# Causal attention in a macaron block: diagonal maxima as packed banks, and q and k loaded in two steps

## The reference

```
scores = jnp.einsum('bhsd,bhtd->bhst', q, k) * scale
causal = jnp.triu(jnp.ones((S, S), dtype=bool), k=1)
scores = jnp.where(causal, -jnp.inf, scores)
probs = jax.nn.softmax(scores, axis=-1)
out = jnp.einsum('bhst,bhtd->bhsd', probs, v)
```

## Time and profile before

| what | us |
|---|---|
| median of 3 runs (1600.67 to 1618.32) | 1615.71 |
| the profiled execution | 1608.4 |
| its span, first to last instruction | 1606.7 |
| PE busy, 8384 matmuls | 1381.6 |
| DVE busy | 1139.5 |
| ACT busy | 860.6 |
| plain maxima on DVE (L1026), 768 | 490.8 |
| masked maxima on DVE (L1031), 512 | 238.3 |
| finds on PE (L1112), 1280 | 478.9 |
| scores on PE (L1133), 1280 | 327.3 |
| products on PE (L1150), 2560 | 322.4 |
| exponentials on ACT (L1001), 640 | 542.7 |

### The profile page before, as it was taken

How to read it: one execution, slowest core, us unless ns; L and a number is a source line. 1 busy time by engine, 2 the same in 40 slices (tenths; PEclk the granted TensorE clock), 3 DMA queues, 4 the chain that set the end, 5 groups by cost and what they waited for, 6 DMA issues and landing times. The chain is left out here.

```text
span 1606.7 us, 27137 instructions
## 1 busy us (share of the span) xinstructions
PE 1381.6 (86%) x8384; PEld 821.8 (51%) x8384; DVE 1139.5 (71%) x2689; ACT 860.6 (54%) x1155; POOL 229.9 (14%) x206
## 2 busy tenths in 40 slices
PE   5988888750799999999999989999999976899997
PEld 5877777640443343343343333433433422799986
DVE  5666676821788888877887887888888930567675
ACT  5644444310036666655665665666666655466564
POOL 0012222346001011010010110110110101110100
PEclk9999999875568899997997999999999978899999
DMA  5113333437152062070080260440620002222312
GB/s 204 40 40 105 105 118 100 150 123 95 13 69 34 6 83 24 5 101 8 9 98 5 30 82 5 55 52 6 72 34 5 8 8 68 92 80 92 95 51 66
DMA packets 101898, 97.86 MB, mean 61 GB/s; under 512 B 46288, under 2 KB 85200, under 8 KB 100048
## 3 DMA queue, kind: packets, MB, share of 16 engines
q1 hardware_dynamic: 101744, 95.98, 29.0%
HBM read 57.15 MB, written 37.75 MB: 59 GB/s over the span
## 5 line engine op out<-in xcount | busy, mean ns | idle before, releaser
L1001 ACT ACTIVATE probs<-s_ps 128x1024 f32<-128x1024 f32 (+3 forms) x640 | 542.7, 895 | 327.7 <-PE s_ps L1133 326.4
L1112 PE MATMUL m_ps<-kT,qT 64*128 64x512 f32 (+3 forms) x1280 | 478.9, 478 | 112.9 <-DMA qT<-qkT_parts 55.9
L1026 DVE TENSOR_REDUCE maxes<-m_ps 128x1 f32<-128x512 f32 x768 | 490.8, 684 | 48.5 <-PE m_ps L1112 44.2
L1112 PEld LDWEIGHTS m_ps<-kT,qT 64*128 64x128 f32 x1280 | 217.2, 201 | 502.2 <-DVE maxes L1026 274.0
L1133 PE MATMUL s_ps<-qT,kT 64*128 64x512 f32 (+3 forms) x1280 | 327.3, 416 | 13.8 <-DMA qT<-shiftT 10.5
L1031 DVE CUSTOM_DVE_ANT_0 masked<-m_ps,mask_b 128x384 f32<-128x384 f32 (+3 forms) x512 | 238.3, 488 | 130.6 <-PE m_ps L1112 125.0
L1150 PE MATMUL o_ps<-probs,v_w 128*32 128x512 f32 (+3 forms) x2560 | 322.4, 578 | 0.2 <-POOL probs L974 0.2
L974 POOL TENSOR_SCALAR_AFFINE_SELECT probs<-probs 128x512 f32<-128x512 f32 x128 | 81.6, 637 | 851.8 <-ACT probs L1001 851.8
L1133 PEld LDWEIGHTS s_ps<-qT,kT 64*128 64x128 f32 x1280 | 164.2, 198 | 41.0 <-ACT probs L1001 25.0
L313 ACT ACTIVATE relu_a<-ups_a 128x512 f32<-128x512 f32 x64 | 38.1, 596 | 100.8 <-PE ups_a L562 99.9
L1150 PEld LDWEIGHTS o_ps<-probs,v_w 128*32 128x32 f32 x2560 | 51.9, 111 | 76.5 <-issue 58.9
(11 more groups left out here) (124 smaller groups left out, 1917.7 us busy)
## 6 DMA issues: line engine op xcount, KB each, us to landing
kT<-qkT_parts SPq DMA_DIRECT2D x48, 256.0 KB
qT<-qkT_parts SPq DMA_DIRECT2D x96, 128.0 KB
qkT_parts<-qk_hi_a SPq DMA_DIRECT2D x32, 256.0 KB, 3.0
qkT_parts<-qk_lo_a SPq DMA_DIRECT2D x32, 256.0 KB, 3.4
qT<-shiftT SPq DMA_DIRECT2D x512, 1.0 KB
xin_a<-in_x SPq DMA_DIRECT2D x8, 512.0 KB, 4.0
xres_a<-in_x SPq DMA_DIRECT2D x8, 512.0 KB, 4.9
x<-xsum_a SPq DMA_DIRECT2D x8, 512.0 KB, 3.2
```

What stands on the lines that cost most here:

```text
L1001: act.activation(probs[:, b % PBUF, 2 * hp:2 * hp + 2, off:CH], s_ps[hp][:, :, off:CH], ACT.Exp, scale=D ** -0.5)\
L1026: dve.tensor_reduce(out, m_ps[:, bank, 0:width], AX.X, ALU.max).then_inc(max_read, 1)
L1112: pe.matmul(m_ps[:, bank, 0:width], qT[of % 2][r0:r0 + HR, j, h // 2, t * P:(t + 1) * P], kT[of % 2][r0:r0 + HR, h // 2, k * CH:k * CH + w ...
```

## The change

Each head and query chunk had four masked units. It now has three plain ones: TRI, a bank of four 128-column triangles, into which PE first multiplies the identity with four copies of the mask in bf16 and then adds the scores of each tile with its own diagonal block; WIDE, two rectangles of 256 columns (tiles 2 and 3); NARROW, two of 128 columns (tiles 1 and 3). DVE takes one segmented plain maximum of each, with 4, 2 and 2 results. A group has 144 units instead of 160, the diagonal ones last in their chunk and no longer in between. The wait for the unit before goes, and so does the tile of masked values. The tile of maxima has six columns instead of four and is filled with a large negative number at the start. SyncE loads terms 0 and 1 of the next group at chunk 0 and term 2 at chunk 1, nothing at chunk 2. The mask's load waits for nothing; PE waits at the start for the bf16 copies of mask and identity.

```diff
-        mask = sb("mask_b", [P, CH])
-        masked = sb("masked", [P, 2, CH])
-        maxes = sb("maxes", [P, 2, G, T, NJ])
+        mask = sb("mask_b", [P, P])
+        masks, identb = sb("masks", [P, T, P], BF16), sb("identb", [P, P], BF16)
+        maxes = sb("maxes", [P, 2, G, T, FULL + NJ - 1])
...
-        UNITS = [(j, t, 2 * hp + par, k, CH if k < j else P * (t + 1))
-                 for j in range(NJ) for t in range(T) for hp in range(G // 2) for k in range(j + 1) for par in range(2)]
+        def diagonal(j, h):
+            k0 = j * CH
+            return [(j, h, [(t, t * P, k0 + t * P, P) for t in range(T)], CH, slice(0, T), TRI),
+                    (j, h, [(2, 0, k0, 2 * P), (3, 2 * P, k0, 2 * P)], CH, slice(2, 4), WIDE),
+                    (j, h, [(1, 0, k0, P), (3, P, k0 + 2 * P, P)], 2 * P, slice(1, 4, 2), NARROW)]
+
+        UNITS = []
+        for j in range(NJ):
+            UNITS += [(j, 2 * hp + par, [(t, 0, k * CH, CH)], CH, slice(t, t + 1), FULL + k)
+                      for t in range(T) for hp in range(G // 2) for k in range(j) for par in range(2)]
+            UNITS += [diagonal(j, 2 * hp + par)[part] for hp in range(G // 2) for part in range(3) for par in range(2)]
...
-            cost = [u[4] + 110 for u in UNITS]
+            cost = [u[3] + 110 for u in UNITS]
...
-            sp.wait_ge(mask_ok, 1)
-            sp.dma_start(mask[:, CH - P:CH], w["mask"]).then_inc(const_in, 16)
+            sp.dma_start(mask[:, :], w["mask"]).then_inc(const_in, 16)
...
-                if j < 3 and exists(i, dn + 1):
+                if j < 2 and exists(i, dn + 1):
...
-                    load(i, dn + 1, (j,))
+                    load(i, dn + 1, ((0, 1), (2,))[j])
...
-            dve.memset(mask[:, :], 0.0).then_inc(mask_ok, 1)
+            dve.memset(maxes[:, :, :, :, :], NEG).then_inc(neg_fill, 1)
             dve.wait_ge(const_in, 32)
+            dve.tensor_copy(masks[:, :, :], mask[:, :].unsqueeze(1).broadcast_to([P, T, P])).then_inc(mask_ok, 1)
+            dve.tensor_copy(identb[:, :], ident[:, :]).then_inc(mask_ok, 1)
+            dve.wait_ge(neg_fill, 1)
...
-                out = maxes[:, j % 2, 2 * (h % 2) + h // 2, t, k:k + 1]
-                if k < j:
-                    dve.tensor_reduce(out, m_ps[:, bank, 0:width], AX.X, ALU.max).then_inc(max_read, 1)
-                else:
-
-                    dve.wait_ge(max_read, done - 1)
-                    dve.sem_inc(passed_max, 1)
-                    dve.tensor_tensor_reduce(masked[:, u % 2, 0:width], m_ps[:, bank, 0:width], mask[:, CH - width:CH], 1.0, NEG,
-                                             ALU.add, ALU.max, out).then_inc(max_read, 1)
+                out = maxes[:, j % 2, 2 * (h % 2) + h // 2, tiles, column]
+                dve.tensor_reduce(out, m_ps[:, bank, 0:width].rearrange("p (n c) -> p n c", n=out.shape[1]), AX.X, ALU.max)\
+                   .then_inc(max_read, 1)
...
+                if column == TRI:
+                    pe.matmul(m_ps[:, bank, :], identb[:, :], masks[:, :, :].rearrange("p t k -> p (t k)"), start=True, stop=True)
                 r0 = HR * (h % 2)
-                pe.matmul(m_ps[:, bank, 0:width], qT[of % 2][r0:r0 + HR, j, h // 2, t * P:(t + 1) * P],
-                          kT[of % 2][r0:r0 + HR, h // 2, k * CH:k * CH + width], start=True, stop=True)\
-                  .then_inc(max_done, 1)
+                for t, c0, k0, keys in pieces:
+                    mm = pe.matmul(m_ps[:, bank, c0:c0 + keys], qT[of % 2][r0:r0 + HR, j, h // 2, t * P:(t + 1) * P],
+                                   kT[of % 2][r0:r0 + HR, h // 2, k0:k0 + keys], start=(column != TRI), stop=True,
+                                   skip_group_check=True)
+                mm.then_inc(max_done, 1)
...
-            pe.wait_ge(const_in, 32)
+            pe.wait_ge(mask_ok, 2)
```

More of the change, by code:

```diff
@@ L696, in attention_phase @@
         HR, MB = P // 2, 3
+        TRI, WIDE, NARROW, FULL = 0, 1, 2, 3
         qT = [sb(f"qT{p}", [P, NJ, G // 2, CH], F32R) for p in range(2)]
@@ L726, in attention_phase @@
         mask_ok, bias_in = sem("mask_ok"), sem("bias_in")
-        passed, passed_max = sem("passed_b"), sem("passed_max")
+        passed, neg_fill = sem("passed_b"), sem("neg_fill")
         o_read, denom_done, att_out = (sem(n) for n in ("o_read", "denom_done", "att_out"))
@@ L1015, in _ @@
                 dve.memset(kT[0][HR * par + HR // 2:HR * (par + 1), :, :].bitcast(F32), 1.0).then_inc(ones_ok[0], 1)
[L1016 removed]
+            dve.memset(maxes[:, :, :, :, :], NEG).then_inc(neg_fill, 1)
             dve.wait_ge(const_in, 32)
+            dve.tensor_copy(masks[:, :, :], mask[:, :].unsqueeze(1).broadcast_to([P, T, P])).then_inc(mask_ok, 1)
+            dve.tensor_copy(identb[:, :], ident[:, :]).then_inc(mask_ok, 1)
+            dve.wait_ge(neg_fill, 1)
             def unit(i, dn, x, ahead, u):
[L1021 removed]
+                j, h, _, width, tiles, column = UNITS[u]
                 done, bank, _ = ring(i, dn, x, (ahead, u))
                 dve.wait_ge(max_done, done + 1)
[L1024 to L1032 removed]
+                out = maxes[:, j % 2, 2 * (h % 2) + h // 2, tiles, column]
+                dve.tensor_reduce(out, m_ps[:, bank, 0:width].rearrange("p (n c) -> p n c", n=out.shape[1]), AX.X, ALU.max)\
+                   .then_inc(max_read, 1)
                 return done + 1
@@ L1105, in find @@
                 of = dn + ahead
-                j, t, h, k, width = UNITS[u]
+                j, h, pieces, _, _, column = UNITS[u]
                 if u == 0:
```

3 lines of the change are left out of this document (1 added, 2 removed).

## The result

The kernel after takes 1646.51 us, the median of 4 runs (1641.56 to 1653.62), against 1611.97 us for the kernel before in 4 runs beside them: a ratio of 1.0225, 95% interval 1.0153 to 1.0298. It is slower, by about 35 us; the forecast was 1641 us, slower. The profiled execution took 1641.56 us, 33 us more than that of before.

A forecast was written before the change was run, and what follows sets the result against it. It took DVE to set the pitch of plain slots, with neither DVE nor PE alone the bound, and chunk 3 waiting for its shift. Terms -20 + 42 + 9 - 1 + 3 + 3.5 - 4.5 = +32 on 1608.4; forecast 1641 us, range 1584 to 1670.

The forecast's parts named there:

- packed banks, groups 1 to 6: Attention slots of groups 1 to 6: fewer, wider maxima, PE's extra work mostly hidden; -3.3 us a group, -20 in all.
- the loads, groups 1 to 6: Start of chunk 2, groups 1 to 6: shift lands behind the earlier load, chunk 2 starts at +36; +42 us.
- clock behind the loads, slots 12-19: After the wait at chunk 2: PE's clock falls; 1.5 us a group, +9 us.
- start and prologue: Before attention's first score: no memset wait, -1 us; triangle pairs cost PE more at half clock, +3 us.
- group 0: First group: slots 0 to 3 at half clock, +3.5 us; the rest of it, -4.5 us.
- well over 12: SyncE's queue, a sign of being right: the 16 shift transfers of chunk 2 take well over 12 us.
- 5 to 9 us: First score of chunk 2, a sign of being right: PE waits 5 to 9 us for the shift in groups 1 to 6.
- the shift's wait under 2 us: First score of chunk 2: PE's wait for the shift under 2 us would show the forecast wrong.
- A, transfers that slip past: Shift of chunk 2: small transfers slip past the loads, slot pitch decides; 1589 us, down to 1575; chance 0.24.
- B, only the issue: Start of chunk 2: the wait is only the issue's, start at +31; 1601 us, up to 1622; chance 0.18.
- C, a queue that holds a dozen: SyncE issues only as room comes: chunk 2 at +40, clock stays low behind it; 1680 us; chance 0.10.
- D, slower triangle slots: Slots with triangle banks 1 us longer, four-unit slots keep 2.7 us; 1629 us without any queue; chance 0.08.

The follow-up runs named there:

- e1: Kernel after (packed banks) with the three-step load of the kernel before, one term at each of chunks 0, 1 and 2: 1620.4 us, ratio 1.0093.
- e2: Kernel before (masked units) with only the two-step load of the change: 1647.8 us, ratio 1.0253.
- e7: e2 with two output tiles used in turn, so DVE does not wait for the output's store: 1646.8 us, ratio 1.0262.
- e4: e1 without the matmul of the mask, so the triangles' maxima include masked keys: 1568.75 us, ratio 0.9775.
- e9: e1 with the mask's matmul on the 64 array rows of its own head only, so half the queries are masked: 1578.5 us, ratio 0.9826.
- e6: e4 with the pieces of a pair's two heads issued in turn, after waiting for both banks: 1581.8 us, ratio 0.9845.
- e5: Kernel before with its masked maxima made plain ones of the same widths, masked keys included: 1596.71 us, ratio 0.9940.
- e3: Kernel after with load term 2 issued two slots later, behind the shift of chunk 2: 1645.0 us, ratio 1.0234.
- e11: e1 with all maxima placed four slots earlier: 1664.9 us, ratio 1.0359.
- e12: Kernel before with all maxima placed four slots earlier: 1641.6 us, ratio 1.0227.
- e13: e10 with two output tiles used in turn: 1590.7 us, ratio 0.9897.
- e10: e4 with all maxima placed four slots earlier: 1623.6 us, ratio 1.0093.

## Why the prediction was right, and where it was not

The side, the size (1641 us against 1646.5) and the mechanism of the loads were right. The packed banks had the wrong sign, and the agreement of the sums is luck: two terms were off by some 30 us each, in opposite senses. In profiled executions:

| term | forecast | measured |
|---|---|---|
| packed banks, groups 1 to 6 | -20 | +13 (e1: 114.5 against 112.3, x 6) |
| the loads, groups 1 to 6 | +42 | +22 (after against e1: 3.6 x 6) |
| clock behind the loads, slots 12-19 | +9 | 0 (25.1 against 25.4 in e1) |
| start and prologue | +2 | -1 |
| group 0 | -1 | 0 |
| sum | +32 | +34 (the profiled executions: +33) |

**The loads: the mechanism right, the size halved.** The forecast was that the shift sits behind the load's data, drained at +34, and that chunk 2 starts at +36. The issue began at +17.0 to +20.4 (forecast +18) and took 10.8 to 11.6 us, not "well over 12"; the last row landed at +34.1 to +35.3, and chunk 2 started at +34.3 to +35.6. What was mis-sized is how much of that time was free. At full clock the forecast's +28.1 for a chunk 2 without the step is right: in e1 it is +28.4 in three groups and +31.2 in one with the loop's jump, and the step costs these four 6.4, 6.0, 6.3 and 4.4 us (forecast 7.9, with the jump 5.2). In the other two, 2 and 6, e1 itself stands at half clock in slots 0 to 3 and starts chunk 2 at +35.0 and +35.3: there the step costs +0.4 and -1.0. So 3.8 us a group were lost on average. In the kernel before, e2 shows the step alone, and there it is +41 us by the ratio, the forecast's size. The prediction also looked for all of it in the shift's wait ("5 to 9 us" in groups 1 to 6); it was under 2 us in every one of them. Two rows of PE's timeline of the kernel after, in one group, show what it found instead, one wait for the store's sake and one for the shift's:

```profile
596.32 0.50 PE L1125 MATMUL m_ps<-kT,qT 64*128 64x512 f32 x1 [3.14 <-DVE att L1079]
...
606.62 0.50 PE L1147 MATMUL s_ps<-qT,kT 64*128 64x512 f32 x2 [1.52 <-DMA qT<-shiftT]
```

The shift's wait is small where the store's lies in front of it, or slow slots 0 to 3; e7 shows that the two waits replace each other. The extra clock loss of 9 us did not come behind chunk 2; but slots 4 to 11 had a clock of 0.93, 0.93 and 0.86 in the three groups with the store's wait, which is inside the +22.

**The packed banks: the step that failed.** The prediction took 1.25 us of PE per head with the two heads one behind the other, 15 us a group more than before, and then said that most of it hides; by stages it made -3.3 us a group of that, with the matmul of the mask in it. It was +2.2 in e1. e4 and e9 name what failed: without that matmul the same banks give -4.1 us a group (108.2 against 112.3), so the hiding holds for everything but the mask. The prediction counted the mask with the 0.21 us of its own columns; in the trace 0.32 us go by before the next piece starts, the other head's side stands, and a bank with two scores takes 1.20 us where its parts add up to 0.94 (0.21, four pieces of 0.13, 0.21 for a pair of scores). From e1 to e4 it is 52 us over 128 of them, 0.4 us each, of which some 10 us are the half clock of slots 0 to 3.

By stage, slots 0 to 3 were put at 9.2 and are 9.8 at full clock, but in three of the six groups the clock stood at half for 10.2 us of them and they took 14.0; 28 to 39 were put at 30.7 and are 32.9; 12 to 19 were put at 23.3 and are 24.1 at full clock in e1. Slots 28, 29 and 30 took 3.2, 3.6 and 3.4 us, 2.1 us more than three slots of four plain maxima. The first two have two triangle banks each and are 0.6 to 0.7 us shorter without the mask (e4: 2.5 and 2.9); slot 30 has none of them, but five banks (two plain, one wide, two narrow), and keeps its 3.4 in e4; in e6 it takes 2.9. The pieces of one head start 0.11 to 0.17 us behind one another in most cases, near the 0.13 that was taken from the transposes.

**DVE.** The segmented maximum of 512 columns took 691 ns against the 684 taken, and the plain line grew by 204 us, not 220. DVE lost 35 us of busy time, but the masked maxima's work and waits were worth only about 10 us of the kernel's (e5), and without the masking DVE waited for PE as long as before, 132.5 us against 130.0. 88.1 us of waits stood beside work that would have set the pitch anyway.

**The rivals.** A, transfers that slip past: not seen, the shift landed behind the load. B, only the issue: refuted as a mechanism, for the issue ended up to 3.8 us apart (+28.2 to +32.0) and the rows landed within 1.2 us of one another at the drained load; in size the 22 us are nearer to its 12 than to the 42, because the half clock had spent part of the time already. C, a queue that holds a dozen: not seen; the 16 transfers were issued in 11.63 us, as before. D, slower triangle slots: in part right. It is where the first term went wrong by 33 us, though by less than its 1 us a slot; of the 2.8 us by which slots 0 to 3 exceed the forecast, 2.1 are the clock and 0.7 the banks.

What the prediction said would show it wrong, the shift's wait under 2 us, did happen, in all six groups, and would have misled: the 3.8 us a group were there, in the store's wait and in slots already slow. The reliable sign was the other one, the start of chunk 2 near +36.

**What stays open.** Why PE's clock stands at half in slots 0 to 3 of some groups. It is so in the kernel after (groups 2, 3, 5), e1 (2, 6), e3 (2, 3, 4) and for 6.8 us in e6, and in no inner group of e4, e9, e2, e5, e7 or of the kernel before. e11, which has the mask's matmul but only plain maxima in slots 0 to 3, has it in no inner group either; e12, without packed banks, has 3.4 us of it in one. So it goes mostly, but not only, with the mask's matmul in these slots. PE is busy throughout in those slots in the kernel after, 14.00 of 14.00 us. No run tells what decides which group it is.

## What to carry to other kernels

Before a load is moved, write down what is issued behind it in the same queue and who waits for that, small transfers first: here 16 transfers of 1 KB and one store, both due at a fixed slot, made a load earlier by one chunk into a loss of 21 to 41 us. When work is moved from one engine to another, price it by what it stops there as well as by its own length: a matmul on all array rows among matmuls on half of them cost 50 us for 54 us of busy time, when the masking that it replaced had cost 10. And ask whether the step is needed: a softmax shift doesn't have to leave out masked keys as long as the exponentials keep their range, and without the mask the packed banks are 2.3% faster than the kernel before.

## What the runs showed of the hardware that was not expected

The loop's jump takes 2.0 to 3.1 us of issue in the kernels before and after, e1, e2, e4, e5, e6 and e9, where the DMA share of the stretch is 0.34 or less, and up to 9.45 us where a load is in flight: 7.14 and 7.33 in e3, 7.81 and 7.90 in e11, 9.41 and 9.45 in e13. The share alone doesn't set it: e10 has 3.35 and 3.88 us at 0.52 and 0.40, e12 2.49 and 2.60 at 0.48 and 0.56, e7 4.17 and 6.02 at 0.72 and 0.37. The packets of the "instruction" queues in the stretch are slow where the jump is slow: 0.3 to 0.6 us each on average where it takes 3.1 us or less (e12: 0.6 and 0.9), 0.5 and 0.7 in e10, 0.9 to 1.3 in e3, e11 and e13, 1.9 and 2.6 in e7. These are the windows of the jump in e4 and in e13, columns as in the stages:

```profile
690.70:692.90 2.20, 0.10 (x1) 0.00 (x0) 0.69 (x1) 0.00 (x0) 2.20 (x2) 0.95 0.34 67
```

```profile
705.00:714.50 9.50, 0.12 (x1) 0.00 (x0) 0.73 (x2) 0.00 (x0) 2.58 (x2) 0.62 0.68 75
```

Once the 512 KB of v are issued, the queue takes nothing more until some 8 us (7.6 to 8.7) behind v's own start, and whatever comes next is shown as held. In the kernel after that is a transfer of a term for 7.25 us (v at 691.13, free at 699.01), in e10 the store of the output for 6.60 (938.58 and 946.19), in the prologue before 8.21. In the kernel before only the last 1.83 us of it fell on the store, at 811.58 behind v at 805.13; in e1 the store is issued 8.6 us behind v and takes 0.41. The Trainium skill, "DMA: Bandwidth & Descriptors", section Queues, rings and completion order, says that completion is not first in, first out for one issuing engine. No run here shows a small transfer that overtakes the load to any use: in the kernel after the shift's last row landed with the drained load in all six groups, 3.3 to 6.6 us behind the end of its issue.

As to the jump, the same section says that a DMA engine takes the queues for which it has work in turn, a packet at a time; by that, instructions in a queue of their own would be held by single packets of the load and not by all of it. The 9.4 us in e13 neither show nor exclude this, as no view tells when the instructions were asked for.
